# Two-layer graph network on one core: table fills, edge keys, attention order and block-wise normalisations changed together

## What is computed

```python
xn = layernorm(x)
# layer 0: graph attention. q2, k2, v2 are two chained projections of xn each.
mask = full(-inf); mask[src, dst] = softplus(edge_type_weights)[type - 1]   # the last of equal edges counts
attn = softmax(q2 @ k2.T / 8 + mask)            # 16 heads of 64
x = x + (attn @ v2) @ wo.T + bo + linear_attention(xn) @ Wo.T + b
x = x + moe(layernorm(x))                       # top 2 of 8 experts, 1024 -> 2*352 -> 1024
xn = layernorm(x)
# layer 1: e = exp(-leaky_relu(al[src] + ar[dst])), summed over all edges (multiplicity counts)
x = x + elu(segment_sum(e * h[dst], src) / rowsum) + (layernorm(attend(xn) @ W_fc + xn) * gamma + beta)
x = x + moe(layernorm(x))                       # 1 of 8 experts, 1024 -> 512 -> 1024
```

## Time and profile before

| | |
|---|---|
| median of three runs | 1174.99 us |
| the profiled execution | 1174.65 us |
| its span, first to last instruction | 1172.7 us |
| PE busy | 1022.6 us (87%) |
| DVE, ACT, POOL busy | 338.6, 210.9, 321.3 us |
| mean granted TensorE clock | 0.932 |

### The profile page before, as it was taken

One profiled execution on the slowest core, in us unless ns is written; L12 is line 12 of the kernel. 1 busy time (PEld: TensorE's weight loads), 2 busy tenths in 40 slices (PEclk: granted clock), 3 DMA queues, 4 the chain that ended last, 5 costly groups with the idle time before them and its releaser, 6 DMA issues.

```text
span 1172.7 us, 10287 instructions
## 1 busy us (share of the span) xinstructions
PE 1022.6 (87%) x3516; PEld 560.6 (48%) x3516; DVE 338.6 (29%) x911; ACT 210.9 (18%) x443; POOL 321.3 (27%) x250
## 2 busy tenths in 40 slices
PE   5999999999999977899659999369999999834983
PEld 4566566565555434444356565134444554323331
DVE  5035252083000466301241010230220554282002
ACT  2122411111110266300111111110111100011420
POOL 3288888888888400000000000100000000000300
PEclk9999999999999999999859999779999999955996
DMA  9844434444444500032507987352332022395894
GB/s 282 174 105 91 108 90 92 105 90 90 108 91 107 206 19 1 18 108 82 186 18 251 356 332 279 144 210 95 107 96 101 19 81 81 112 354 179 331 349 164
DMA packets 62252, 170.44 MB, mean 145 GB/s; under 512 B 22144, under 2 KB 22656, under 8 KB 62080
## 3 DMA queue, kind: packets, MB, share of 16 engines
q1 hardware_dynamic: 36832, 140.53, 35.6%
q0 software_dynamic: 21632, 17.94, 8.7%
q10 hardware_dynamic: 3744, 11.42, 2.8%
HBM read 156.39 MB, written 13.47 MB: 145 GB/s over the span
## 4 chain that ended last, share of the span: by engine, by line
PE 51%; POOL 23%; DMA 8%; issue 8%; DVE 7%; ACT 2%; ACTq 0%; DVEq 0%; POOLq 0%
PE bank L920 21%; POOL n_hi L487 7%; POOL n_lo L487 7%; PE bank L1127 7%; POOL w_lo L487 4%; POOL w_hi L487 4%; PE bank L909 4%; PE bank L1152 4%; DMA n_hi<-G 3%; PE bank L1350 3%; PE bank L1333 3%; PE bank L1029 1%; PE bank L901 1%; PE bank L1265 1%; DMA Y<-xs,idx 1%
## 5 line engine op out<-in xcount | busy, mean ns | idle before, releaser
L909 PE MATMUL bank<-xnT,ring 128*128 128x384 f32 x896 | 292.7, 487 | 1.5 <-ACT xnT L646 0.9
L909 PEld LDWEIGHTS bank<-xnT,ring 128*128 128x128 f32 x896 | 169.7, 190 | 119.6 <-ACT xnT L646 1.1
L540 POOL DMA_INDIRECT Y<-xs,idx x12 | 11.4, 953 | 613.9 <-DMA xs<-Y 297.9
L920 PE MATMUL bank<-ring,Y 128*128 128x512 f32 x384 | 166.5, 593 | 0.8 <-DVE Y L1863 0.8
L920 PE MATMUL bank<-ring,xnT 128*128 128x512 f32 x288 | 124.0, 592 | 0.6 <-ACT xnT L631 0.6
L920 PEld LDWEIGHTS bank<-ring,Y 128*128 128x128 f32 x384 | 72.5, 190 | 92.9 <-issue 90.7
L487 POOL DMA_INDIRECT n_hi<-count,ridx x48 | 83.8, 1746 | 14.6 <-issue 14.3
L920 PEld LDWEIGHTS bank<-ring,xnT 128*128 128x128 f32 x288 | 54.6, 190 | 68.9 <-issue 67.9
L487 POOL DMA_INDIRECT n_lo<-count,ridx x48 | 83.3, 1736 | 14.6 <-issue 14.6
L909 PE MATMUL bank<-Y,ring 128*128 x256 | 82.7, 486 | 0.0
L1127 PE MATMUL bank<-ring,Y 128*128 128x352 f32 x256 | 78.9, 467 | 0.7 <-issue 0.7
(11 more groups left out here) (266 smaller groups left out, 1012.2 us busy)
## 6 DMA issues: line engine op xcount, KB each, us to landing
ring<-in_stream SPq DMA_DIRECT2D x144, 512.0 KB
ring<-in_up SPq DMA_DIRECT2D x32, 704.0 KB, 5.7
Y<-in_stream SPq DMA_DIRECT2D x18, 512.0 KB, 10.0
G<-in_stream SPq DMA_DIRECT2D x16, 512.0 KB, 12.1
ring<-in_dn SPq DMA_DIRECT2D x7, 1024.0 KB, 5.6
ys<-Y ACTq DMA_DIRECT2D x12, 512.0 KB, 7.2
xnT<-in_stream SPq DMA_DIRECT2D x6, 512.0 KB
Y<-in_dn SPq DMA_DIRECT2D x7, 384.0 KB, 6.8
```

Of the source, the lines that this page charges most:

```text
L540: pool.indirect_dma_start(dst, None, src, bass.IndirectOffsetOnAxis(ap=idx[:, col:col + 1], axis=0))\
L909: last = pe.matmul(bank[to][:, 0:N], ring[:, r, k * P:(k + 1) * P], rhs(k), start=(k == 0), stop=(k == KB - 1))
L920: last = pe.matmul(bank[2 + 3 * half + b][:], lhs(k0 + k, b), ring[:, r, k * 512:(k + 1) * 512], start=(start and k == 0), stop=(stop and ...
```

## The change

1. **Early fills.** The four tables are filled by SP, between the loads of ring slots 1 and 2, in place of POOL. The wait for x and the constants goes.
2. **Keys from DRAM.** POOL also makes the key rows (96 rows of 128) from a second copy of `src` and `dst` in row form, which ACT loads as its fifth DMA, and stores them to `keys` in DRAM. POOL now waits for both copies before it does anything with edges. The first layer's keys stay on PE (`first_keys`). For layers two to six SP loads them, broadcast to all partitions, into `rows` (two DMAs of 512 KB for each layer), and `dedup` reads them there in place of PSUM. The load of the biases `bo_g`, `bo_m` into the same tile moves behind the last dedup.
3. **Attention order.** A pair's `apply` moves behind the next pair's start; the two `turn`s stand together. DVE and ACT follow.
4. **Block-wise normalisations.** The second halves of the output projection and of `fc` run block by block (`block_rows`), so that blocks 0 and 1 are finished early; each block is added, normalised, transposed (8 tiles) and given its logits on its own. The same without the matmuls after the first experts. After `fc` the rows go to `xs` block by block, before ACT's wait for the logits.
5. `load_b2(0)` no longer waits for `zf_done`; two semaphores become one.

```diff
@@ SP
+            for r in range(2):
+                load(r, r)
+            sp.wait_ge(blanked, 2)
+            for table, blank in ((w_lo, absent), (w_hi, absent), (n_lo, none), (n_hi, none)):
+                sp.dma_start(table[0:TABLE, :].rearrange("(p m) a -> p (m a)", p=P), blank).then_inc(filled, 16)
+                sp.dma_start(table[TABLE:TABLE + P, :], blank[:, 0:1]).then_inc(filled, 16)
+            for r in range(2, SLOTS):
+                load(r, r)
+            def load_keys(layer):
+                for q in range(2):
+                    sp.dma_start(rows[:, q, :].rearrange("p (t n) -> p t n", t=GT_),
+                                 keys_d[bass.ds((layer + HG * q) * GT_, GT_), :].unsqueeze(0)
+                                 .to_broadcast([P, GT_, P])).then_inc(key_rows_in, 16)
...
+            sp.wait_ge(keys_stored, 16)
+            load_keys(1)
...
+            with sp.Fori(2, HG) as g:
                 for r in range(SLOTS):
-                    sp.wait_ge(chunk_used, 8 * g - 7 + r)
-                    load(r, 8 * g + r)
+                    next_chunk(g, r)
+                    if r == 3:
+                        sp.wait_ge(edges_ready, 2 * g + 2)
+                        load_keys(g)
...
-            sp.wait_ge(zf_done, 6)
             load_b2(0)
@@ POOL
-            pool.wait_ge(edge_in, 16)
+            pool.wait_ge(edge_in, 32)
...
-            pool.wait_ge(x_in[NB - 1], 16)
-            pool.wait_ge(k_in, 48)
-            for table, blank in ((w_lo, absent), (w_hi, absent), (n_lo, none), (n_hi, none)):
...
+            pool.tensor_copy(key_row, edge_rows[:, 0, :])
+            step(pool.tensor_copy(key_dst, edge_rows[:, 1, :]))
+            step(pool.tensor_scalar(key_row, key_row, float(N), None, ALU.mult))
+            step(pool.tensor_tensor(key_row, key_row, key_dst, ALU.add))
+            pool.dma_start(keys_d, key_row).then_inc(keys_stored, 16)
@@ ACT
+            act.dma_start(edge_rows, erows_d).then_inc(edge_in, 16)
...
-            seed(1)
-            act.wait_ge(xn_ready, 2 * NB)
-            store_rows(xn)
-            evict_transposes(T_LN2, TP0, xnT)
+            for b in range(NB):
+                seed(1 + b, b, b + 1)
+                act.wait_ge(xn_ready, NB + b + 1)
+                store_block(xn, b)
+                evict_block(TP0, b)
...
+            seed(13)
+            for b in range(NB):
+                act.wait_ge(xh_ready, b + 1)
+                store_block(YN(2), b)
             act.wait_ge(act_input, AF)
             act.activation(w[:, 24:48], w[:, 216:240], ACT.Sigmoid).then_inc(act_output, 1)
-            act.wait_ge(xh_ready, NB)
-            store_rows(YN(2))
@@ PE
+            def block_rows(b, slots, lhs, arrived, start, stop):
+                for r in slots:
+                    if b == 0:
+                        pe.wait_ge(landed[r], arrived)
+                    for k in range(2):
+                        last = pe.matmul(bank[5 + b][:], lhs(2 * (r % 4) + k, b), ring[:, r, k * 512:(k + 1) * 512],
+                                         start=(start and r == slots[0] and k == 0),
+                                         stop=(stop and r == slots[-1] and k == 1), skip_group_check=True)
+                    if b == NB - 1:
+                        last.then_inc(chunk_used, 1)
+                if b < NB - 1 and stop:
+                    last.then_inc(block_done, 1)
...
             def layer_A(layer, before=None):
-                if not isinstance(layer, int) or layer:
-                    keys(layer)
...
             for p in range(HP):
-                for a in range(2):
-                    turn(p, a)
-                    if 3 * p + 5 + a < UNITS:
-                        scores(3 * p + 5 + a)
-                apply(p)
-                if 3 * p + 7 < UNITS:
-                    scores(3 * p + 7)
+                if p:
+                    apply(p - 1)
+                if 3 * p + 5 < UNITS:
+                    scores(3 * p + 5)
+                turn(p, 0)
+                turn(p, 1)
+                for g in (3 * p + 6, 3 * p + 7):
+                    if g < UNITS:
+                        scores(g)
+            apply(HP - 1)
...
+            for b in range(NB):
+                block_rows(b, mix_slots, tok(2), arrived, True, False)
+                if b:
+                    turn_block(T_LN2, NB, b - 1)
+                block_rows(b, gnn_slots, tok(4), arrived, False, True)
+                if b:
+                    if b == 1:
+                        pe.wait_ge(x1_done, NB)
+                    logits(T_LN2, wqkv, 3 * NE, b - 1)
+            turn_block(T_LN2, NB, NB - 1)
+            logits(T_LN2, wqkv, 3 * NE, NB - 1)
@@ DVE
+                elif q == 0:
+                    v.wait_ge(key_rows_in, 32 * layer)
...
+                    src = (bank[4 + 2 * q + t // 4][:, (t % 4) * P:(t % 4 + 1) * P]
+                           if isinstance(layer, int) and layer == 0 else rows[:, q, t * P:(t + 1) * P])
...
+            for b in range(NB):
...
+                tt(z3[:, b, 512:1024], bank[5 + b][:], xn[:, b, 512:1024], ALU.add).then_inc(zf_done, 1)
+                v.wait_ge(zf_done, NB + b + 1)
+                step(half_stats(z3, b, 1))
+                aggregate(b)
+                rstd_of(7 + 2 * b, b, b + 1)
                 step(stt(z3[:, b, :], z3[:, b, :], mv[:, b, 0:1], rows[:, 0, :], ALU.subtract, ALU.mult))
                 step(stt(xr[:, b, :], z3[:, b, :], rstd[:, b:b + 1], xr[:, b, :], ALU.mult, ALU.add))
-            rstds(4, xr)
-            normalise(xn, xr, xn_ready)
+                half_stats(xr, b, 0)
+                step(half_stats(xr, b, 1))
+                aggregate(b)
+                rstd_of(8 + 2 * b, b, b + 1)
+                normalise_block(xn, xr, b, xn_ready)
```

339 lines of the change are left out of this document (165 added, 174 removed).

## The result

The changed kernel takes 1133.12 us (median of 4 runs, 1129.68 to 1133.83), the kernel before 1175.62 us on the same chip (1174.73 to 1179.8): a ratio of 0.9619 with a 95% interval of 0.9586 to 0.9651. The profiled execution took 1129.68 us, of which 1127.9 are the span; the forecast for these was 1130 and 1128.

The account below looks back on a forecast made before the run. PE was taken to set the pace, with waits in the attention and at three normalisations. Terms -1 + 0 - 17 - 11 - 1 - 14.5 = -44.5 took 1174.65 to 1130 us; 8-in-10 range 1115 to 1149.

Parts of the forecast that it names:

- Start and layers A: PE's path to v2: 10 us of key matmuls removed, against a later start and chunk three at 40; -1 us.
- The mask's path: POOL's scatters start 12 us earlier, dedups add 5 us; mask ready at 394.4, PE needs it at 402; cost 0.
- Attention: First transposes to output projection: seven pairs each lose 2.45 us of PE waits, pairs take 7.3 us; -17 us.
- Output projection and router: Last output matmul to first router logits: blocks finished early, 13.3 us in place of 24.3; -11 us.
- After the first experts: Normalisation there: last block 3 us later on DVE, but 16 of 24 transposes no longer behind it; -1 us.
- After `fc`: From `fc`'s end to the gather: DVE blocks of 9.4 us, gather at +32 against +47.7; -14.5 us.
- both late paths: Late chunk three puts the start at +7 us; POOL held up by the whole 22 us of dedup costs 9 us.
- Harmless small writes: Rival: small writes do no harm at the start, which gains 6 instead of 1, with full attention clock; 1122 us, chance 0.22.
- Late mask: Rival: late chunk three or POOL held up by dedups, 7 to 10 us more, 1139; chance 0.24 including a slower pair.
- slower than before: Rival: key loads stretch scatter landings past the 6.4 us round, paid 48 times; 1185 us at 1.3 us each; chance 0.03.

Follow-up runs that it names:

- pads_one_row: Changed kernel with each table's 128 spare words written as one 512-byte row from one partition instead of 128 four-byte writes: 1129.92 us, ratio 0.9627.
- late_fills: Changed kernel with the eight table fills moved back from SP to POOL, behind the arithmetic on the edges: 1129.00 us, ratio 0.9593.
- before_chunks_held: Kernel before with one wait added on SP, so layer two's chunks load only when all table fills have landed: 1175.81 us, ratio 1.0004.
- fc_halves: Changed kernel with layer 2's last product in two halves of all blocks, all three blocks normalised at once, transposes by block: 1141.17 us, ratio 0.9719.
- casts_early: Changed kernel with a separate semaphore for the edge rows, so POOL's first casts do not wait for them: 1130.45 us, ratio 0.9630.

## Why the prediction was right, step by step

**Start and layers A** (-1 forecast, -3.9 at v2, -3.2 at the attention). The parts fell as described: layer one at 24.26 (24), the fifth DMA landed just ahead of 13.19 (12.5), five sets of key matmuls gone. Only the fills' landing was 2 to 3.5 us too late in the forecast: chunk three let PE go on at 36.59, not at 40. That the jam comes from the small writes, which was an assumption, is shown by `pads_one_row`. The forecast's own sum has the two delays hide in each other: with chunk three at 40, PE's start at 24 costs nothing more. In the run the chunk came sooner, so both count: 4.4 + 1.75 - 10 = -3.9.

**The mask's path** (cost 0 forecast, 0 measured). POOL started at 36.27 (39), and the mask was ready at 391.2 (394.4), with 7 us to spare ahead of the third unit's scores. The charge of 5 us for dedups with two operands in SBUF was not paid: the 192 scatters sum to 269.2 us where they summed to 270.2 before, beside 80 such dedup operations of 351 ns. So the first pair of the earlier trace rows, a scatter stretched to 4.73 us, comes with one long operation of 3.36 us, and does not carry over to short ones: beside the dedups at 178 to 184 and 220 to 226 us no scatter is stretched. The Trainium skill, GPSIMD Engine Reference, section 1, says that GpSimd and VectorE instructions with two SBUF inputs contend; for operations as short as these this trace shows none of it. The reason given for the 12 us, early issue and less traffic beside the fills, was wrong in its weight: early issue makes 4.4 of 15.1 us (`late_fills`), and the larger share is that layer two's chunks no longer run beside the fills (7.6 us, measured in the kernel before by `before_chunks_held`). It hid behind a right total since nothing waits for the mask.

**Attention** (-17 forecast, -21.6). Mechanism and bound as forecast: PE-bound pairs of 6.94 us (7.3). The term was undersized by 4.6 us, and what failed is the price of a pair, 7 x 2.45, which counted idle time alone. Over the whole stretch PE's idle time fell from 15.9 to 0.9 us, so 14.9 and not 17 came from the waits, and its busy time fell from 56.8 to 50.1, 6.6 us that the sum left out. Two things make these. Timeline of the kernel before on PE, a turn and a unit's scores in one pair and in the next:

```profile
444.38 1.20 PE L1015 MATMUL bank<-k,G 128*128 128x128 f32 x9 [1.81 <-DVE G L1540]
445.51 0.92 PE L1000 MATMUL bank<-Y 64*128 64x384 f32 x4
...
453.84 2.14 PE L1015 MATMUL bank<-k,G 128*128 128x128 f32 x9 [1.82 <-DVE G L1540]
455.91 1.61 PE L1000 MATMUL bank<-Y 64*128 64x384 f32 x4
```

and of the changed kernel, two units' scores in one go:

```profile
448.46 1.56 PE L1039 MATMUL bank<-Y 64*128 64x384 f32 x8
```

The 0.92 of the earlier trace rows is a mean. From 454 to 456 us the clock is 0.50, and the turn and the scores there take 1.6 us more; this happens three times in the stretch (at 433.3, 453.8 and 474.4, in every second pair, though the wait of 1.8 us stands ahead of all of them) and comes to 4.8 us. In the changed kernel, with hardly any waits, the clock stays at 1.00 from the first transposes to the projection. The rest is mostly the scores: two units in one go take 1.56 us, and apart 2 x 0.92, 0.3 us less in each pair. The forecast had priced the full clock at 3 us and left it out.

**Output projection and router** (-11 forecast, -10.6). The last product ended 3.5 us later after the start (4.5), and the router's copy came 10.2 us behind it (13.3 - 4.5 = 8.8).

**After the first experts** (-1 forecast, -1.0 with the 0.6 lost in the gathers). In layer 1, which was taken as unchanged, 2.1 us were lost: the 288 matmuls of `chunk_N` on `xnT` take 601 ns on the mean in place of 592. The clock shows why. Windows of 20 us from the first layer-1 matmul, of the changed kernel:

```profile
742.37:762.37 20.00, 20.00 (x42) 8.81 (x43) 0.00 (x0) 0.00 (x0) 0.00 (x0) 0.89 0.30 103
```

and of the kernel before:

```profile
778.73:798.73 20.00, 20.00 (x47) 9.00 (x48) 0.00 (x0) 0.00 (x0) 0.00 (x0) 1.00 0.24 79
```

Before, PE did its 24 transposes in one go, at a clock of 0.50, and came to layer 1 at full clock. Now they are done a block at a time, at 0.50 too, with waits of 4.3 us between, and layer 1's matmuls still run at 0.50 to 0.52 until 747 us. No run undid this step alone, so that the waits are the cause is read from the two windows and not tested.

**After `fc`** (-14.5 forecast, -10.6; +N is N us behind PE's last `fc` matmul, at 988.85). DVE's blocks took 9.3 us (9.4) and the router's copy came at +23.6 (22.7), so the mechanism held. The failed term is "the gather can start at +32": it started at +35.2, since `xs` stores took 9.0 us to land in place of 8.1, and then needed 7.5 us in place of 5.7. The forecast named the cause, chunk loads beside them, but its price was too low: from +47.7 to +32 are 15.7 us, of which it took 14.5, so 1.2 for the loads against 5.0 measured (3.2 at the start of the gather, 1.8 in it). With the last loads held, the gather starts at +31.5, when its indices are ready. `fc_halves` confirms the size of the whole step (10.75 at the first up product).

Two errors, +4.6 in the attention and -3.9 after `fc`, cancel, and so do +2.2 at the start and -2.1 in layer 1. That the total, 44.5 against 44.8, came out this close is luck; the mechanisms held, two of their prices did not. One sum of the forecast does not come out either: its terms' bounds add up to 1117 and, with both late paths counted, 1161, not 1113 and 1158.

**Rivals.** Harmless small writes: they are not harmless, but their harm is 2 us (without them v2 begins 0.9 us earlier from a start 1.1 us later). Late mask and slower than before: scatters waited for landings only 5.0 and 2.5 us in all at the two count tables, and key loads landed in 5.6 us in the median.

## What to carry to other kernels

Where three engines pass a tile round, look at what the engine that sets the pace has to do while the others work on its next input: moving one product of the pair before into PE's gap was worth 17 to 20 us, and the order of the engines that had slack did not matter. Waits of such an engine can cost more than their own length: here 6.6 of the 21.6 us won were busy time, 4.8 of them from the clock. When a wait is removed and nothing changes, read the trace for the wait that takes its place before dropping the edit: at the first scores `pads_one_row` was worth 0.9 us alone, `casts_early` -0.4, and both together 4.1. And holding loads back for the sake of another transfer moved the collision to the next transfers here rather than removing it.

## What the runs showed that was not expected

Writes of four bytes, 128 to a DMA, cost far more than their bytes: 2 KB of them in the queue of 2.3 MB of fills held the engines at 117 GB/s from 20 to 30 us, against 342 GB/s with four rows of 512 bytes, and the unrelated store of 48 KB behind them took 16.4 us in place of 5.1. A fill's landing depended more on which chunk loads were allowed beside it (7.6 us) than on when it was issued (13 us earlier gave 4.4 us). Also, an indirect gather of 512 KB issued behind eleven loads of 512 KB, with eight more behind it, had landed only 21.8 us after its issue, while in the changed kernel the second gather let PE go on 4.4 us after it was issued.
